# A four-layer gated network on one core: the third attention's weights are requested in the layer before, and the two layers share one set of blocks

## The reference, cut to what matters

```python
# fourth: h = silu(x wg) * (x wu), for two of 8 experts, and for the shared one
shared = jax.nn.silu(xt @ sg_w.T) * (xt @ su_w.T) @ sd_w.T
routed = jnp.einsum('te,teh->th', w, y)
...
# fifth: encoder_hc = layernorm(x), decoder_hq = context
w1, w2, w3 = (w_sim[:d], w_sim[d:2 * d], w_sim[2 * d:])
Sim = (encoder_hc @ w1)[:, :, None] + (decoder_hq @ w2)[:, None, :] + \
      jnp.einsum('bid,bjd->bij', encoder_hc * w3, decoder_hq) + b_sim[0]
A = jax.nn.softmax(Sim, axis=2)
hq_hat = jnp.einsum('bij,bjd->bid', A, decoder_hq)
Batt = jax.nn.softmax(jnp.max(Sim, axis=2), axis=1)
hc_bar = jnp.einsum('bi,bid->bd', Batt, encoder_hc)[:, None, :]
hc_hat = jnp.broadcast_to(hc_bar, encoder_hc.shape)
feats = jnp.concatenate([encoder_hc, hq_hat, encoder_hc * hq_hat, encoder_hc * hc_hat], axis=-1)
hcq = feats @ W_qv + b_qv
```

## Time and profile before

| what | value |
|---|---|
| median of 3 executions | 1744.58 us (1744.38 to 1750.98) |
| the profiled execution, its own time | 1746.42 us |
| its span, first to last instruction | 1744.6 us |
| TensorE busy | 1391.7 us (80%) |
| VectorE busy | 1152.3 us (66%) |
| ScalarE busy | 935.2 us (54%) |
| GpSimd busy | 755.8 us (43%) |
| mean granted clock of TensorE | 0.910 of full speed |

### The profile page before, as it was taken

One profiled execution on the slowest core, in us unless ns is written; L12 is line 12 of the kernel. 1 busy time (PEld: TensorE's weight loads), 2 busy tenths in 40 slices (PEclk: granted clock), 3 DMA queues, 4 the chain that ended last, 5 costly groups with the idle time before them and its releaser, 6 DMA issues. The chain is left out here.

```text
span 1744.6 us, 31848 instructions
## 1 busy us (share of the span) xinstructions
PE 1391.7 (80%) x10246; PEld 1183.6 (68%) x10246; DVE 1152.3 (66%) x2511; ACT 935.2 (54%) x2046; POOL 755.8 (43%) x797
## 2 busy tenths in 40 slices
PE   2588878999999999877784779999758925463898
PEld 0344455899999999734464779999756822152687
DVE  6456665688888888467765568787553448777554
ACT  4245542777777777456632357777425326355332
POOL 2322202466666666412220058888302920135444
PEclk8799998999999999899995889999889967685999
DMA  4000004455656565220013036667410010011001
GB/s 161 10 1 2 1 22 176 144 217 207 226 200 234 190 243 182 90 69 1 1 49 118 39 111 222 220 213 221 129 46 1 2 53 1 1 31 56 1 13 37
DMA packets 62368, 171.87 MB, mean 99 GB/s; under 512 B 11760, under 2 KB 43248, under 8 KB 53056
## 3 DMA queue, kind: packets, MB, share of 16 engines
q1 hardware_dynamic: 53440, 146.50, 24.2%
q0 software_dynamic: 8832, 24.13, 4.3%
HBM read 152.25 MB, written 18.35 MB: 98 GB/s over the span
## 5 line engine op out<-in xcount | busy, mean ns | idle before, releaser
L1706 POOL TENSOR_TENSOR l0m_e_DL<-l0m_e_DN,l0m_e_DH 128x256 fp32r<-128x256 f32 x184 | 182.1, 995 | 121.3 <-ACT l0m_e_DH L1545 75.0
L1489 PE MATMUL PS<-l0m_e_CH,l0m_e_UH 128*128 128x256 f32 x736 | 210.9, 287 | 2.0 <-DVE l0m_e_CL L1639 2.0
L1489 PE MATMUL PS<-l0m_e_CH,l0m_e_UL 128*128 128x256 f32 x736 | 208.9, 284 | 0.0
L1489 PE MATMUL PS<-l0m_e_CL,l0m_e_UH 128*128 128x256 f32 x736 | 208.9, 284 | 0.0
L1611 DVE TENSOR_TENSOR l0m_e_UL<-l0m_e_U,l0m_e_UH 128x512 fp32r<-128x512 f32 x184 | 149.0, 810 | 10.4 <-ACT l0m_e_UH L1536 10.4
L1489 PEld LDWEIGHTS PS<-l0m_e_CH,l0m_e_UH 128*128 128x128 f32 x736 | 141.9, 193 | 2.2 <-ACT l0m_e_UH L1536 2.2
L1489 PEld LDWEIGHTS PS<-l0m_e_CL,l0m_e_UH 128*128 128x128 f32 x736 | 142.0, 193 | 0.0
L1489 PEld LDWEIGHTS PS<-l0m_e_CH,l0m_e_UL 128*128 128x128 f32 x736 | 141.9, 193 | 0.0
L1623 DVE SCALAR_TENSOR_TENSOR Z<-PS,l0m_e_BU,Z 128x256 f32<-128x256 f32 x184 | 88.7, 482 | 73.4 <-ACT Z L1553 71.0
L1553 ACT ACTIVATE Z<-PS,l0m_e_BU 128x256 f32<-128x256 f32 x184 | 87.6, 476 | 83.4 <-PE PS L1489 83.3
L1536 ACT CAST l0m_e_UH<-l0m_e_U 128x512 fp32r<-128x512 f32 x184 | 113.1, 615 | 0.0
(11 more groups left out here) (531 smaller groups left out, 4534.8 us busy)
## 6 DMA issues: line engine op xcount, KB each, us to landing
l0m_e_U<-in_l_up SPq DMA_DIRECT2D x23, 2048.0 KB
l0m_e_DN<-in_l_down SPq DMA_DIRECT2D x23, 1024.0 KB, 4.9
l1m_e_U<-in_l_up SPq DMA_DIRECT2D x23, 1024.0 KB, 7.6
l1m_e_DN<-in_l_down SPq DMA_DIRECT2D x23, 512.0 KB, 3.9
CTX<-in_ctx SPq DMA_DIRECT2D x2, 2048.0 KB, 10.4
l1a_GA<-results_by_choice SPq DMA_DIRECT2D x16, 256.0 KB, 5.8
l1m_c_GA<-results_by_choice SPq DMA_DIRECT2D x16, 256.0 KB, 3.0
Z<-in_l_b_rows SPq DMA_DIRECT2D x23, 128.0 KB, 3.0
```

The costliest lines, as they stand in the source:

```text
L1489: ins = nc.tensor.matmul(hb(f)[:, a * SLOTS:(a + 1) * SLOTS], w[:, f % RING, k, a, :], x[:, j, k, :], start=(p == 0), stop=(p == len(passe ...
L1706: nc.gpsimd.tensor_tensor(DL[:, f % RING, :], DN[:, j, f, :], DH[:, f % RING, :].bitcast(F32), ALU.subtract).then_inc(s_dl, 1)
```

## The change

Four of the five arrays, WC, W1, BS and WQ, get their tiles on a stack of their own (`ahead`) when `l1_moe` begins, so that they lie under its tiles and live until the attention is done; the tiles of `l1_moe` move up by 8,384 bytes a partition for it (8,192 of WQ, 128 of W1, 32 each for WC and BS). SyncE requests them inside `Combine.load`, after the first eight requests for routed results, with WQ first. They count up a semaphore of their own, to 64. BQ stays in the attention's block, alone, with a semaphore of its own. VectorE waits for BQ where it waited for all five, and gets a wait for the 64 before it first reads BS. `l1_moe` and `l2_attention` become steps of one layer, so that the `end_layer()` between them is gone; the clearing after the attention now covers the semaphores of both.

```diff
+        ahead = ExitStack()
+        l2 = {}
+
+        def l2_tiles():
+            for name, shape in (("WC", [P, 3, KD]), ("W1", [P, KD, 4, 4]), ("BS", [P, 1]),
+                                ("WQ", [P, 4 * KD, D])):
+                l2[name] = sb_in(ahead, f"l2a_{name}", shape)
+            l2["loaded"] = sem("l2a_loaded")
+
+        def l2_load(sp):
+            for tile, array in ((l2["WQ"][:, :, :], I["L2_xattn_W_qv"].rearrange("(k p) n -> p k n", p=P)),
+                                (l2["WC"][:, :, :], I["l2_wsim_cols"]), (l2["W1"][:, :, :, :], I["l2_w1_columns"]),
+                                (l2["BS"][:, :], I["l2_bsim_rows"])):
+                sp.dma_start(tile, array).then_inc(l2["loaded"], 16)
...
                 for b in range(B):
+                    if b == self.RING:
+                        l2_load(sp)
                     if b >= self.RING:
                         sp.wait_ge(self.s_used, 2 * (b - self.RING + 1))
...
         def l1_moe():
+            l2_tiles()
...
                     @block.sync
                     def _(sp):
-                        for tile, array in ((WC[:, :, :], I["l2_wsim_cols"]), (W1[:, :, :, :], I["l2_w1_columns"]),
-                                            (BS[:, :], I["l2_bsim_rows"]), (BQ[:, :], I["l2_bqv_rows"]),
-                                            (WQ[:, :, :], I["L2_xattn_W_qv"].rearrange("(k p) n -> p k n", p=P))):
-                            sp.dma_start(tile, array).then_inc(s_ld, 16)
+                        sp.dma_start(BQ[:, :], I["l2_bqv_rows"]).then_inc(s_bq, 16)
...
-                        pe.wait_ge(s_ld, 80)
+                        pe.wait_ge(s_ld, 64)
...
-                        act.wait_ge(s_ld, 80)
+                        act.wait_ge(s_ld, 64)
...
                         def best(g):
                             dve.wait_ge(s_max, GROUP * (g + 1))
+                            dve.wait_ge(s_ld, 64)
...
-                        dve.wait_ge(s_ld, 80)
+                        dve.wait_ge(s_bq, 16)
                         nc.vector.tensor_scalar(BQ[:, :], BQ[:, :], GATES[:, 2:3], None, ALU.mult).then_inc(s_gb, 1)
...
-        layers = ((lambda: layernorm("l0x_ln", have_stats=True), decay_layer), (l0_attention, l0_moe, l1_attention), (l1_moe,),
-                  (l2_attention,), (l2_ffn,), (l3_attention,), (l3_ffn,))
+        layers = ((lambda: layernorm("l0x_ln", have_stats=True), decay_layer), (l0_attention, l0_moe, l1_attention), (l1_moe, l2_attention, ahead.close), (l2_ffn,), (l3_attention,), (l3_ffn,))
```

More of the change, by code:

```diff
@@ L2132, in l2_attention @@
                 new_zt(c)
[L2133 to L2136, removed]
+                WC, W1, BS, WQ = (l2[n] for n in ("WC", "W1", "BS", "WQ"))
                 BQ = sb_in(c, "l2a_BQ", [P, D])
+                s_ld = l2["loaded"]
                 ZW = sb_in(c, "l2a_ZW", [P, KD, T])
@@ L2150, in l2_attention @@
                 HC = sb_in(c, "l2a_HC", [P, KD, B])
-                names_ = ("loaded", "steps", "var", "sd", "rstd", "z_dve", "z_act", "ctx_w", "ctx_w_copied", "turned",
+                names_ = ("bias", "steps", "var", "sd", "rstd", "z_dve", "z_act", "ctx_w", "ctx_w_copied", "turned",
                           "zt", "zw", "scores", "max", "exp", "recip", "scaled", "e_turned", "et", "hq", "cq",
@@ L2154, in l2_attention @@
                           "bar", "hc", "wb", "out", "x", "gated_bias", "xb", "stats")
-                (s_ld, s_st, s_var, s_sd, s_ok, s_zd, s_za, s_g, s_gc, s_tr, s_zt, s_zw, s_s, s_max, s_exp, s_rec,
+                (s_bq, s_st, s_var, s_sd, s_ok, s_zd, s_za, s_g, s_gc, s_tr, s_zt, s_zw, s_s, s_max, s_exp, s_rec,
                  s_sc, s_etr, s_et, s_hq, s_cq, s_mf, s_mt, s_bm, s_be, s_brec, s_bs, s_bt, s_ba, s_bar, s_hc, s_wb,
```

## The result

| | before | changed |
|---|---|---|
| median of 8 executions | 1744.22 us | 1735.64 us |
| lowest and highest | 1739.75, 1750.98 | 1730.32, 1741.58 |
| profiled execution's span | 1744.6 us | 1733.2 us |

The ratio of the changed kernel to the one before is 0.9948, with a 95% interval from 0.9928 to 0.9968: 9.1 us faster, between 5.6 and 12.6. Measured a second time, it was 0.9942 (0.9920 to 0.9963). The prediction was 1734.2 us, in a range of 1731 to 1739.

The account below looks back on a forecast made before the run. Blocks run in sequence, so the wait for WQ at the third attention's head enters the span in full. Boundary 1.0 plus wait 9.35 gives 10.35 us off 1744.58: 1734.2 us, range 1731 to 1739 (forecast's own 1732.5 to 1735.3).

Parts of the forecast that it names:

- The wait and where it goes: At the third attention's start, TensorE's wait for WQ goes, so its first product starts 9.35 us earlier.
- TensorE's path: First context product to first turn at the attention's start: 9.35 us earlier by WQ, 10.35 us with the layer boundary.
- The boundary in front: Routed layer to attention: the 1.44 us gap becomes a plain 0.33 us step, saving 0.8 to 1.1, taken as 1.0.
- The clearing behind: At the merged layer's end, clearing more semaphores is still two instructions, so costed at nothing; upper bound another 1.1 us.
- The short path and BQ: Attention's start: ScalarE and VectorE gain only 8.4 us but block 0 is still in time; BQ's later request costs 0.
- The slack: Time from normalised block 0 being ready to TensorE's first turn: shrinks from 2.66 to 0.7 us, and holds.
- The clock: At the attention's start TensorE begins at half clock for the same 5.5 us, as work and order are unchanged.
- Rival 2: TensorE's full clock returns sooner at the attention's start: gain 11.5 us (1733.1), or 13.0 (1731.5) if at once; chance 0.14.
- The gathers: In the shared expert's block, the four requests before the ninth gather of routed results cost nothing; VectorE does not wait.
- The cover: Ninth gather lands at 1264, VectorE first uses it at 1271.01: seven microseconds remain.
- The median: Whole kernel: 1744.58 us, the median of the runs shown, less 10.35 gives 1734.2 us, 0.6% faster.
- rival 1: At the attention's start, block 0 or BQ comes later than TensorE, or half clock lasts longer: gain 8.4 to 9.3; chance 0.22.

## Why the prediction was right

**The wait and where it goes.** Right: 9.35 us was predicted for TensorE's path by the requests alone, and the wait from the opening on fell from 9.35 us to nothing with them alone; for both it was 10.35 against 10.47 (10.79 to 0.32 us after the last statistics). That the size fits so well is in part luck. It is the wait in the one profile that the prediction was read from, and the same requests in their old place cost 8.76 and 7.32 us in two others. The prediction took that one profile for every execution.

**The boundary in front.** Predicted 1.0, between 0.8 and 1.1; 1.11 measured (1.44 to 0.33).

**The clearing behind.** This is the term that was mis-sized: "it is still two instructions, so I cost it at nothing". It is two instructions, but the gap grows by 0.0069 us for each semaphore, and 84 more of them cost 0.58 us. The bound of 1.1 us held. The merging is thus worth 0.53 us over its two ends, about a twentieth of the whole, and with the 0.44 us that come at the next layer's end, 0.09 us: next to nothing.

**The short path and BQ.** TensorE's path did set the start. The slack was reckoned from the matmul of the turn (0.7 predicted, 0.64 measured); from the weight load, which needs block 0 as well, it was 0.21 us. BQ took 3.7 us to land and came 0.48 us late, where the prediction took 2.0. In the changed kernel's second profile it took 2.1 us and nobody waited, so neither row was the right one: it differs between executions. The Trainium skill's fit (DMA: Bandwidth & Descriptors, Anatomy of one DMA) gives 2.3, near the 2.1 and far from the 3.7; the section states it for transfers that GpSimd requests, and this one is SyncE's, which I had left out of account. The late BQ cost the copy of the first turned block 0.1 us, and requesting it early changed the length by 0.2.

**The clock.** The half clock lasted 5.6 us in the profile of the result, 5.5 were predicted. That was not given by the work and its order, as the prediction argued: with the same work it lasted 2.9 us in the second profile. Rival 2, that an earlier full clock would give 1 to 3 us more, was right about the start and, by the ten profiles, about its price; what it left out is that the clock fell again in all four profiles in which it had risen before 3 us, and in none of them was the attention shorter.

**The gathers.** No wait, as predicted, though the landing grew from 3.0 to 5.0 us. The cover was larger than reckoned: with five times the bytes the wait was 2.16 us.

**The median.** 10.35 was predicted from one profile, 9.8 is what the two profiles show in the stretch that the change touches, and the medians say 8.6 (by the ratio 9.1, 10.1 the second time). These agree within the interval. The 9.8 are 9.35 and 1.11 less 0.58 and less 0.08 by which the attention was longer. The measured median, 1735.64, lies in the stated range, but 0.3 us outside the forecast's own (1732.5 to 1735.3) and where rival 1 was to be; it is the rows above, not the time, that decide against rival 1 (of which only BQ's 0.1 us came true). Nor is it shown that the change is faster by over 0.5%, to which the prediction gave 0.71: the gain is 0.52%, between 0.32 and 0.72. What blurs them is the routed layer: from ScalarE's first cast for the shared expert to the block with the gathers it took 279.6 us in the profile of before, 279.9 in that of the changed kernel, and 273 to 279 in the experiments' profiles. Part of this goes with ScalarE's waits for the experts' weights, 22.3 and 23.6 us in those two, 8.3 in the run with the requests behind the gathers (273.1 us); but one run with 273.7 us had 18.4, so the cause isn't settled.

## What to carry to other kernels

Where every stage starts from a barrier, a weight load that is waited for at the stage's head costs its whole issue and flight (7.3 to 9.4 us here, from one execution to another), and moving its request one block up gives all of it back; any place behind the transfers that the block itself is waiting for will do. Then check which engine is second at the head: here the normalised block was 0.2 us from setting the start, and with TensorE's products made faster it did set it. A merged layer doesn't save the clearing of its semaphores, only the fixed part of one layer's end, and the ends behind it have to be looked at too: here the next one took most of that back. And a start that gets TensorE's clock up sooner is not worth idle matmuls until the whole stage is seen to be shorter.

## What the runs showed of the hardware

Clearing semaphores has a price per semaphore: a layer's end grew by 6.9 ns for each, linear over 22, 31, 38, 41, 83, 122, 138 and 148, but one end with 41 took 0.44 us more than this in all profiles of the merged kernels, for a reason not found. The same 128 KB load, alone in its queue at the head of its block, took 3.7 us to land in one profile of the changed kernel and 2.1 in another, and the same request, with one value of 4 bytes for each of 128 partitions, held SyncE for 0.43, 1.49 and 1.96 us in three profiles. And TensorE's granted clock fell in the middle of a stage, 36 to 37 us after the stage's start, in the four profiles in which it had risen early, and in none of the ten others, while the engine was at work nine tenths of the time before it fell (3.87 of 4.5 us, 3.76 of 4.2). Why the early rise should lead to it was not found.
